# Tridiagonalisation of a 1024 x 1024 Laplacian: kappa from unscaled products, the reflector's pair in two operations, and the norm taken right behind the new column

## The reference

```python
def _L2_gnn_ref(features, A, W1, b1, W2, b2):
    ...
    L = jnp.diag(deg) - A
    L_norm = d_inv_sqrt[:, None] * L * d_inv_sqrt[None, :]
    _, U = jnp.linalg.eigh(L_norm)
    agg = jnp.einsum('mn,bnd->bmd', U.T, features)
    h = jax.nn.relu(agg @ W1 + b1)
    out = h @ W2 + b2
    return jnp.einsum('nm,bmd->bnd', U, out)
```

## Time and profile before

| | |
|---|---|
| median of 3 runs | 9881.85 us (9870.64 to 9885.23) |
| the profiled execution's own time | 9871.62 us |
| its span | 9869.9 us |
| busy: TensorE, VectorE, ScalarE, GpSimd | 52%, 72%, 18%, 12% |
| first to last step of the tridiagonalisation | 920 to 6090 us of the span |

### The profile page before, as it was taken

How to read it: one execution, slowest core, us unless ns; L and a number is a source line. 1 busy time by engine, 2 the same in 40 slices (tenths; PEclk the granted TensorE clock), 3 DMA queues, 4 the chain that set the end, 5 groups by cost and what they waited for, 6 DMA issues and landing times. The chain is left out here.

```text
span 9869.9 us, 311313 instructions
## 1 busy us (share of the span) xinstructions
PE 5128.9 (52%) x128994; PEld 3544.3 (36%) x128994; DVE 7105.6 (72%) x33446; ACT 1777.0 (18%) x4691; POOL 1178.6 (12%) x5177
## 2 busy tenths in 40 slices
PE   5675878777777767766654433121111110047856
PEld 2354555555555555554443332010000000033355
DVE  3555666767777776777777778989898989954154
ACT  1432111111111111111111121121111110011054
POOL 0000111111222221222222221000000000000000
PEclk8898999999999777555555555555555555579988
DMA  1000000000000000000000000000000000000000
GB/s 35 1 0 18 4 4 4 4 4 4 4 4 4 4 4 3 4 4 4 4 3 3 3 3 2 0 0 0 0 0 0 0 0 0 0 0 1 17 0 17
DMA packets 24537, 40.99 MB, mean 4 GB/s; under 512 B 2464, under 2 KB 20128, under 8 KB 23200
## 3 DMA queue, kind: packets, MB, share of 16 engines
q1 hardware_dynamic: 23200, 21.70, 0.7%
HBM read 17.50 MB, written 4.19 MB: 2 GB/s over the span
## 5 line engine op out<-in xcount | busy, mean ns | idle before, releaser
L289 PE MATMUL tri_y<-L 128*32 128x256 f32 (+7 forms) x36792 | 2091.7, 366 | 11.9 <-issue 11.6
L289 PEld LDWEIGHTS tri_y<-L 128*32 128x32 f32 x36792 | 1282.2, 132 | 250.7 <-issue 47.9
L1338 PE MATMUL ev_agree<-ev_prod,ev_fold 128*128 128x448 bf16 x520 | 241.5, 568 | 1683.3 <-DVE ev_prod L1461 1666.7
L272 PE MATMUL tri_k<-tri_kp,tri_half 128*32 128x1 f32 x8176 | 270.0, 191 | 1329.4 <-DVE tri_x L472 1329.4
L272 PEld LDWEIGHTS tri_k<-tri_kp,tri_half 128*32 128x32 f32 x8176 | 183.2, 124 | 1695.3 <-DVE tri_x L472 1695.3
L1454 DVE SCALAR_TENSOR_TENSOR ev_seq<-ev_seq,ev_ne2G,ev_u 128x112 f32<-128x112 f32 x2048 | 686.0, 335 | 73.3
L1450 DVE SCALAR_TENSOR_TENSOR ev_u<-ev_x,ev_dG,ev_seq 128x112 f32<-128x112 f32 x2048 | 684.1, 334 | 64.0
L1338 PEld LDWEIGHTS ev_agree<-ev_prod,ev_fold 128*128 128x128 bf16 x520 | 34.6, 111 | 1888.0 <-DVE ev_prod L1461 1867.6
L360 ACT ACTIVATE tri_mu<-tri_ring,tri_tiny 128x1 f32<-128x1 f32 x1022 | 267.1, 261 | 2242.7 <-PE tri_ring L272 2242.7
L272 PE MATMUL tri_ring<-L 128*32 128x32 f32 (+25 forms) x35704 | 639.3, 215 | 0.0
L362 ACT ACTIVATE tri_sM<-tri_half_M,tri_s 128x8 f32<-128x8 f32 (+7 forms) x1022 | 304.3, 298 | 1823.2 <-DVE tri_s L464 1823.2
(11 more groups left out here) (613 smaller groups left out, 12792.4 us busy)
## 6 DMA issues: line engine op xcount, KB each, us to landing
adj<-in_adj_dram SPq DMA_DIRECT2D x12, 1024.0 KB, 8.1
x<-in_x_dram SPq DMA_DIRECT2D x8, 512.0 KB, 7.2
out_dram<-x SPq DMA_DIRECT2D x8, 512.0 KB, 6.6
gcn_w<-in_L_gnn_W_dram SPq DMA_DIRECT2D x2, 128.0 KB, 2.1
spec_w<-in_L_gnn_W_dram SPq DMA_DIRECT2D x2, 64.0 KB, 1.9
dot_wt<-in_L_gnn_W_dram SPq DMA_DIRECT2D x1, 64.0 KB, 1.9
dot_rows<-in_L_gnn_b_lin_dram SPq DMA_DIRECT2D x1, 64.0 KB, 2.7
dot_rows<-in_L_gnn_b_dram SPq DMA_DIRECT2D x1, 64.0 KB, 3.6
```

Of the source, the lines that this page charges most:

```text
L272: last = nc.tensor.matmul(out[32 * g:32 * g + 32, :], lhsT, rhs, start=start, stop=stop)
L289: last = nc.tensor.matmul(y[32 * g:32 * g + 32, 0:T * 32], A[:, b + t, XC:XC + 1].broadcast_to([P, 32]), cols, start=(t == 0), stop=(t == ...
L1338: last = nc.tensor.matmul(agree, fold16[:, :], prod[:, z, h * (GRP // 2):(h + 1) * (GRP // 2), :].rearrange("p s w -> p (s w)"), start=Fal ...
```

## The change

With `few(T)` meaning T of 4 or less, in every step:

1. The pair: `S2` goes. Two operations take its place ahead of the pair, `sgn2` = sigma x sign and `aa` = mu x sign + pivot, both made of what is there with the root; `pair` = rt x sgn2 + aa.
2. `gx` is made ahead of `c4`, and `c4` now comes with its half in one two-column operation (`scale`).
3. kappa. With T of 5 or more it is the sum of two parts: `x4` multiplies the correction with c4 and gx ahead of the transpose, into `kpc`; `x3` reads the transposed product directly, and the sum `tm` is formed behind it. TensorE adds both parts. With T of 4 or less `x3` goes; TensorE sums gx x tm over tiles (T small products in place of one, and T again for `c_sum` with `zh` = tm x c4/2), and the factor c4/2 moves into `vmc` on ScalarE.
4. `q` = qa x c4 + Bc in one operation; `sM` on ScalarE goes, and GpSimd's `nB` becomes `flm` and `hm`, which need the flag alone.
5. The next step's sum of squares (`norm`) stands right behind x, ahead of the column w.
6. TensorE, T of 4 or less: the first product (all of them for T of 2 or 1) stands behind `sigma` and ahead of `rows`; before, T = 4 had it ahead of `sigma`.

```diff
+                        nc.gpsimd.tensor_scalar(flm[:, :], fl[:, s:s + 1], -1.0, None, ALU.add).then_inc(pool_step, 1)
+                        pool.wait_ge(pool_step, 4 * r + 1)
+                        nc.gpsimd.tensor_scalar(hm[:, b:NT], half_M[:, s, 0:T], flm[:, :], None, ALU.mult).then_inc(pool_step, 1)
+                        if s:
+                            pool.wait_ge(Bn_ready, r + 1 if s0 else r)
                         nc.gpsimd.tensor_scalar(fB[:, b:NT], col, fl[:, s:s + 1], None, ALU.mult).then_inc(pool_step, 1)
-                        pool.wait_ge(pool_step, 3 * r + 1)
-                        nc.gpsimd.tensor_tensor(nB[:, b:NT], fB[:, b:NT], col, ALU.subtract).then_inc(pool_step, 1)
-                        pool.wait_ge(pool_step, 3 * r + 2)
-                        nc.gpsimd.tensor_tensor(Bc[:, b:NT], nB[:, b:NT], half_M[:, s, 0:T], ALU.mult).then_inc(pool_step, 1)
+                        pool.wait_ge(pool_step, 4 * r + 2)
+                        nc.gpsimd.tensor_tensor(Bc[:, b:NT], col, hm[:, b:NT], ALU.mult).then_inc(pool_step, 1)
...
-                        early = 0 if T < 4 else 1
-                        for t in range(early):
-                            product(t)
+
+                        first = T if T <= 2 else 1
+                        if not few(T):
+                            for t in range(first):
+                                product(t)
                         pe.wait_ge(norm_part, r + 1)
                         four(sigma, ones[:, 0:32], part[:, :]).then_inc(norm_ready, 1)
+                        if few(T):
+                            for t in range(first):
+                                product(t)
...
-                        for t in range(early, T):
+                        for t in range(first, T):
                             product(t)
-                        pe.wait_ge(kappa_part, r + 1)
-                        four(kappa(s), half[:, 0:32], kp[:, :]).then_inc(kappa_ready, 1)
-                        four(c_sum, half[:, 0:32], kp[:, :], stop=False)
+                        if few(T):
+
+                            pe.wait_ge(gx_ready, r + 1)
+                            pe.wait_ge(t_ready, r + 1)
+                            tm = t1 if s else tr[:, 0:NT * 32].rearrange("p (t m) -> p t m", m=32)[:, :, 0]
+                            t0 = b if s else 0
+                            for t in range(T):
+                                last = four(kappa(s), gx[:, b + t:b + t + 1].broadcast_to([P, 32]), tm[:, t0 + t:t0 + t + 1], start=(t == 0), stop=(t == T - 1))
+                            last.then_inc(kappa_ready, 1)
+                            pe.wait_ge(zh_ready, r + 1)
+                            for t in range(T):
+                                four(c_sum, gx[:, b + t:b + t + 1].broadcast_to([P, 32]), zh[:, b + t:b + t + 1], start=(t == 0), stop=False)
+                        else:
+                            if s:
+                                pe.wait_ge(corr_part, r + 1 if s0 else r)
+                                four(kappa(s), half[:, 0:32], kpc[:, :], stop=False)
+                                four(c_sum, half[:, 0:32], kpc[:, :], stop=False)
+                            pe.wait_ge(kappa_part, r + 1)
+                            four(kappa(s), half[:, 0:32], kp[:, :], start=(s == 0)).then_inc(kappa_ready, 1)
+                            four(c_sum, half[:, 0:32], kp[:, :], start=(s == 0), stop=False)
...
-                        act.wait_ge(s4_ready, r + 1)
-                        nc.scalar.activation(sM[:, b:NT], half_M[:, s, 0:T], ACT.Copy, scale=s4[:, s:s + 1]).then_inc(sM_ready, 1)
                         act.wait_ge(xm_ready, r + 1)
                         act.wait_ge(inv_ready, r + 1)
                         nc.scalar.activation(vm[:, b:NT], xm[:, b:NT], ACT.Copy, scale=inv[:, 1:2]).then_inc(vm_ready, 1)
+                        if few(T):
+                            act.wait_ge(c4_ready, r + 1)
+                            act.wait_ge(vm_ready, r + 1)
+                            nc.scalar.activation(vmc[:, b:NT], vm[:, b:NT], ACT.Copy, scale=s4[:, s, 1:2]).then_inc(vmc_ready, 1)
...
```

VectorE's step, new (the helper functions of the pieces keep their old waits unless shown):

```diff
+                        f1 = fl[:, s:s + 1]; c4 = s4[:, s, 0:1]; c4h = s4[:, s, 1:2]
+                        pre = r + 1 if s0 else r
+                        done = {}
+
+                        def sign():
+                            dve.wait_ge(pivot_ready, r + 1)
+                            done["sg"] = mark(V_.tensor_scalar(sg[:, :], pivot(s)[:, 1:2], 0.0, -0.5, ALU.is_ge, ALU.add))
+
+                        def root():
+                            dve.wait_ge(root_ready, r + 1)
+                            done["rt"] = mark(V_.reciprocal(rt[:, :], mu[:, :]))
+                            V_.tensor_scalar(f1, pivot(s)[:, 1:2], pivot(s)[:, 1:2], sigma, ALU.mult, ALU.is_lt).then_inc(fl_ready, 1)
+                            after(done["sg"])
+                            mark(V_.tensor_scalar(sgn2[:, :], sigma, sg[:, :], None, ALU.mult))
+                            done["a"] = mark(V_.scalar_tensor_tensor(out=aa[:, :], in0=mu[:, :].broadcast_to([P, 2]), scalar=sg[:, :], in1=pivot(s), op0=ALU.mult, op1=ALU.add))
+
+                        def pair_():
+                            after(done["a"])
+                            done["pair"] = mark(V_.scalar_tensor_tensor(out=pair[:, s, :], in0=rt[:, :].broadcast_to([P, 2]), scalar=sgn2[:, :], in1=aa[:, :], op0=ALU.mult, op1=ALU.add))
+
...
+                        def scale():
+                            dve.wait_ge(inv_ready, r + 1)
+                            dve.wait_ge(fl_ready, r + 1)
+                            V_.scalar_tensor_tensor(out=s4[:, s, :], in0=one_half[:, :], scalar=inv[:, 0:1], in1=f1.broadcast_to([P, 2]), op0=ALU.mult, op1=ALU.mult).then_inc(c4_ready, 1)
...
+                        def total():
+                            after(done["tr"])
+                            V_.tensor_tensor(tm, trc, corr[:, act_t], ALU.add).then_inc(t_ready, 1)
+
+                        def masked():
+                            dve.wait_ge(t_ready, r + 1)
+                            done["qa"] = mark(V_.tensor_tensor(qa[:, act_t], tm, (Mw if few(T) else half_M)[:, s, 0:T], ALU.mult))
+
+                        def z_half():
+                            dve.wait_ge(c4_ready, r + 1)
+                            V_.tensor_scalar(zh[:, act_t], tm, c4h, None, ALU.mult).then_inc(zh_ready, 1)
+
+                        def z_():
+                            dve.wait_ge(pool_step, 4 * r + 3)
+                            V_.scalar_tensor_tensor(out=z, in0=tm, scalar=c4, in1=fB[:, act_t], op0=ALU.mult, op1=ALU.add).then_inc(z_ready, 1)
+
+                        def q_():
+                            dve.wait_ge(pool_step, 4 * r + 4)
+                            after(done["qa"])
+                            done["q"] = mark(V_.scalar_tensor_tensor(out=q[:, act_t], in0=qa[:, act_t], scalar=c4h if few(T) else c4, in1=Bc[:, act_t], op0=ALU.mult, op1=ALU.add))
+
+                        sign()
+                        root()
...
+                            g_x()
+                            scale()
+                            dve.wait_ge(gx_ready, r + 1)
+                            dve.wait_ge(c4_ready, r + 1)
+                            if s:
...
+                                V_.scalar_tensor_tensor(out=x4[:, act_t], in0=corr[:, act_t], scalar=c4, in1=gx[:, act_t], op0=ALU.mult, op1=ALU.mult,
+                                                        accum_out=kpc[:, 0:1]).then_inc(corr_part, 1)
+                            turn()
...
+                            V_.scalar_tensor_tensor(out=x3[:, act_t], in0=trc, scalar=c4, in1=gx[:, act_t], op0=ALU.mult, op1=ALU.mult,
+                                                    accum_out=kp[:, 0:1]).then_inc(kappa_part, 1)
+                            if s:
+                                total()
+                            masked()
+                            z_()
+                            q_()
+                            dve.wait_ge(vm_ready, r + 1)
...
+                        if s + 1 < s1:
+                            norm(r + 1)
```

158 lines of the change are left out of this document (91 added, 67 removed).

## The result

The changed kernel took **10212.92 us** (median of 4 runs, 10206.99 to 10226.67) against 9876.24 us (9865.95 to 9885.23) for the kernel before on the same chip: ratio **1.034, 95% interval 1.0325 to 1.0361**. The forecast was 9914 with a range of 9855 to 9985: right in sign, eight times too small. The profiled execution took 10210.05 us with a span of 10208.3, 338 us longer than before's.

The account below looks back on a forecast made before the run. It took the products to bound steps at large T and early in a panel, VectorE's queue otherwise. T of 5 or more +53 us, T of 4 or less -21, clock +10: +42 on 9871.6 makes 9914 us, range 9855 to 9985.

Parts of the forecast that it names:

- The front of T of 5 or more: VectorE's queue ahead of the transpose: pair +0.12 us, kappa's `scale` and `x4` +0.30 us in a queue-bound step.
- The rival that charges full durations: VectorE operations cost their full duration, so `sgn2` and `aa` for `S2` cost 0.20 us, not 0.12: 9970 us; chance 0.07.
- the one in which the additions fit in gaps: VectorE's additions at T of 5 or more fit in gaps, half the loss there: 9885 us; chance 0.18.
- The back of T of 5 or more: From the transpose's end to x: 0.85 us instead of 0.89, a saving of 0.04 to 0.05 us.
- T of 4: Stage T = 4: three more small sets for kappa make its back +0.05 us, sigma comes earlier; +4 us in all.
- Sigma's earlier start: At T = 4, sigma comes about 0.3 us earlier, since the first product no longer stands ahead of it.
- T = 3 to 1: Stages of few tiles: T = 3 gets 5 us shorter, T = 2 and 1 together 20 us shorter.
- Norm's gain: At T = 3 to 1, norm starts 0.11 us earlier and sigma follows it directly: -0.11 us a step.
- the back: At T = 3 to 1, from the transpose's end to x: -0.06 us at T = 3, -0.10 at T = 2 and 1.
- The clock: TensorE is less busy in longer steps at T = 6 and 5, so its clock falls 0.04: some +10 us.
- Rival 1: TensorE's clock falls far, T = 6 to T = 5's and T = 5 to T = 4's: 10,004 us, half-way 9950; chance 0.13.
- rival 2: TensorE's clock rises at T = 4 and 3 through more small sets, making the kernel faster: 9856 us; chance 0.12.

Follow-up runs that it names:

- the kernel with 672 us: The changed kernel with few(T) meaning T of 3 or less, so T = 4 takes the path of the larger T: 10301.83 us, ratio 1.043.

## Why the prediction was right in sign and wrong in size

**The front of T of 5 or more: right.** +0.12 for the pair and +0.30 for `scale` and `x4` made 0.42. Measured, in the steps at the higher clock in which the transpose did not wait: +0.39 at T = 6 (3.40 to 3.79 us from x to the transpose) and +0.44 at T = 5 (3.13 to 3.57). The transpose waited for the product in 74, 39 and 29 steps at T = 7, 6 and 5 instead of 93, 54 and 65. So 19, 15 and 36 steps turned from product-bound to queue-bound, where the forecast took 15, 20 and none; the mechanism is the one that was described. The rival that charges full durations fell with that, and so did the one in which the additions fit in gaps. The former rests on a sentence of the Trainium skill, "VectorE: DVE Perf Modes", section "The DRAIN you can't avoid", but that section goes on that an operation that is not held starts earlier, and the starts inside running operations agree with this.

**The back of T of 5 or more: this step failed.** "0.17 + 0.03 to `qa`, 0.08 to `z`, 0.14 to `q` ... + 0.03 to x: 0.85. -0.04 to -0.05." It was +0.12 (0.89 to 1.01), in 495 of 511 steps more than 0.05 above before's median: some 60 us against a saving of some 20. The prediction saw that x would wait for `q` instead of kappa, and priced that hand-over at 0.03, as between two instructions of which the second carries the wait. The wait for `q` was the last of three, in an instruction of its own. With the order turned the same stretch measures 0.85 or 0.86. The stages T = 8 to 5 then differ from before by -6, +40, +44 and +19 us, against -6, +12, +27 and +20 forecast.

**T of 4: this step failed, and by most.** "+0.05" behind the transpose, "+4" in all, against +130. The sets were priced by their slots on TensorE (0.107 us each, which holds: from `kappa` to `c_sum` 32 matmuls take 0.42 us in the rows above), but TensorE had not the instructions. Kappa, `c_sum`, pivot, sigma, rows, coefs and products are 320 instructions that follow each other with short gaps from some 0.7 us ahead of x to 2.6 us behind it. The stops take some 99 of the 130 us. The path was mis-sized too: the steps without a stop are 0.24 us longer than before, some 30 us, where +4 was forecast (and +0.13 and -0.1, half and half, make +2). Sigma's earlier start was right: from x to `rt` it is 1.14 us instead of 1.47. The rows of before could not show it, since T = 4 had no such idle time inside its steps; the number of instructions a step, which could be counted, was given no cost.

**T = 3 to 1**: -25 forecast, -3 measured. Norm's gain is 14 to 17 us a stage, as the 0.11 us said (128 x 0.11 = 14); the pair cost 12 to 15 us a stage, as 0.12 said. What failed is the back: -0.06 at T = 3 and -0.10 below became +0.02, -0.01 and -0.02 in the median. With the waits turned the back is 0.90, 0.85 and 0.81 us (forecast 0.86, 0.82, 0.82).

**The clock**: +10 forecast. It fell by 0.06, 0.07 and 0.02 at T = 7, 6 and 5; by the prediction's own rate of 3.7 us for 0.01 that is an estimate of 55 us. (By the same rate the forecast's fall of 0.04 makes 15 us, not 10.) The direction was right (longer steps, less of TensorE busy), but T = 7 had been left out, and the steps grew by more than was taken. Rival 1, with T = 6 at T = 5's clock, did not come, nor rival 2: T = 4 went from 0.59 down to 0.53.

**The sum.** Of the 331 us, 130 are T = 4 and 204 T = 8 to 5. Of the latter, 107 went when the waits were turned. The 97 left stand against a forecast of 53 and 10 for the clock, with more steps turned at T = 5 and a deeper fall of the clock (0.95 and 0.90 at T = 7 and 6 even then). How the 97 split between the two is not shown. No rival held an instruction stream that runs dry, nor a hand-over that costs more by the order of its waits, and the range had no room for either. That the sign was right is owed to the front; 130 + 107 of the 331 us came with the two steps that failed.

## What to carry to other kernels

Where an instruction of VectorE has several waits, name first in the code the one that comes last: it costs nothing and gave 0.3% here on a tuned kernel, 1.5% on the changed one. Many tiny matmuls are not priced by their slots alone: count the instructions that stand close together (250 and more within some 3 us), and look for "issue" in TensorE's waits; if a step's count is near 256, as at T = 3, a stage can gain or lose a fifth by what stands ahead of its loop, so an experiment that changes the code ahead of a loop is judged by stages, never by the total. In a queue of dependent small operations an operation moved off the chain but into the queue saves nothing.

## What the runs showed of the hardware

- TensorE can run out of instructions in the middle of a run of matmuls. It went on some 2.4 us behind the start of the 16 KB transfer, of which 1.0 us is the transfer itself. The stops lie 254 matmul and load instructions apart at T = 4, and at T = 3, with 257 instructions a step, their place moves back by one a step. The stage of T = 3 took 672, 703, 558 and 558 us for four positions of the border (stops in 87, 124, 0 and 0 steps); the last three were foretold. That is against "mostly hidden" in the Trainium skill's section named above; the block size there agrees. What sets off a transfer was not tried by itself. It starts at 0.40 and 0.44 us behind x in the two kernels that stop, at 1.57 and 0.80 in those that don't, and at 1.9 in the first panel of the kernel with 672 us, whose borders lie as in the panels that stop.
- A VectorE instruction with a wait that comes last in a separate semaphore instruction starts 0.05 to 0.11 us later than with that wait in itself: x starts 0.14 us behind `q`'s end in the one case and 0.03 in the other, `q` 0.19 and 0.14 behind `z`.
- The same number of instructions costs little where TensorE has idle time: 320 a step at T = 4 took 617 us against 608, with 41 stops, and 738 us in one burst, with 71.
- `sgn2`, which reads one PSUM scalar, and `aa` together took 0.25 us of VectorE's queue ahead of the products (0.44 - 0.19), as the estimate of 0.12 and 0.13 had it.
